# Gate and up of a SwiGLU block as a 2x2 block product in seven products (Strassen–Winograd) instead of eight, with every low part on VectorE

## What is computed

```
x: 2048 x 512, float32; attention weights Wq 512 x (16 x 32), Wk and Wv 512 x (16 x 8); gate and up 1792 x 512; down 512 x 1792
xn = (x - mean) / sqrt(var + eps)                       per token
q, k, v = xn Wq + bq, xn Wk + bk, xn Wv + bv
attn    = softmax over e of (q k^T)/4, per token, 16 x 16; s = attn v
nx = xn * rsqrt(mean(xn^2) + eps) * ln_w
g  = silu( ( silu(nx gate^T) * (nx up^T) ) down^T )
out = x + s * g
```

## Time and profile before

| | |
|---|---|
| time, median of three runs | 522.2 us (522.16 to 522.37) |
| span of the profiled execution | 520.4 us |
| instructions | 6685 |
| PE busy (matmuls) | 507.2 us, 97%, 2320 matmuls |
| DVE busy | 374.8 us, 72% |
| ACT busy | 195.1 us, 37% |
| HBM read and written | 25.56 and 7.34 MB |
| mean granted TensorE clock | 0.997 of full speed |

### The profile page before, as it was taken

How to read it: one execution, slowest core, us unless ns; L and a number is a source line. 1 busy time by engine, 2 the same in 40 slices (tenths; PEclk the granted TensorE clock), 3 DMA queues, 4 the chain that set the end, 5 groups by cost and what they waited for, 6 DMA issues and landing times.

```text
span 520.4 us, 6685 instructions
## 1 busy us (share of the span) xinstructions
PE 507.2 (97%) x2320; PEld 424.8 (82%) x2320; DVE 374.8 (72%) x542; ACT 195.1 (37%) x373; POOL 27.5 (5%) x41
## 2 busy tenths in 40 slices
PE   6999999999999999999999999999999999999993
PEld 5888888888888888888888888888888888888882
DVE  6899756876278653886569797686775867588777
ACT  4857862124311234114276575211332114221311
POOL 5030010200102000010000000000000000000000
PEclk9999999999999999999999999999999999999998
DMA  8823350000400004000043212201031010300312
GB/s 269 287 82 102 97 186 0 1 1 2 161 0 0 0 0 161 0 0 0 0 161 102 81 42 81 82 0 40 0 128 74 0 40 0 122 0 1 112 50 81
DMA packets 15168, 33.11 MB, mean 64 GB/s; under 512 B 1456, under 2 KB 2736, under 8 KB 14384
## 3 DMA queue, kind: packets, MB, share of 16 engines
q1 hardware_dynamic: 13200, 22.42, 13.5%
q0 software_dynamic: 1952, 10.49, 5.8%
HBM read 25.56 MB, written 7.34 MB: 63 GB/s over the span
## 4 chain that ended last, share of the span: by engine, by line
PE 95%; DVE 2%; ACT 1%; DMA 1%; SPq 0%; issue 0%; DVEq 0%; ACTq 0%
PE gate_ps L283 29%; PE up_ps L283 29%; PE y_ps L283 29%; PE aux_ps L283 6%; PE aux_ps L367 1%; DMA raw<-gate 1%; DVE raw L702 1%; DVE y_part L697 0%; ACT zT_hi L536 0%; DVE y_part L687 0%; SPq L172 0%; ACT raw L437 0%; DVE h_lo L746 0%; DVE h L738 0%; ACT y_part L526 0%
## 5 line engine op out<-in xcount | busy, mean ns | idle before, releaser
L471 ACT ACTIVATE h_hi<-h 128x512 fp32r<-128x512 f32 x56 | 35.4, 632 | 173.9 <-DVE h L738 159.4
L738 DVE TENSOR_TENSOR h<-h,up_ps 128x512 f32<-128x512 f32 x56 | 38.4, 687 | 79.4 <-PE up_ps L283 76.8
L283 PE MATMUL y_ps<-down_hi,h_hi 128*128 128x512 f32 x224 | 88.4, 395 | 0.3 <-DVE h_lo L746 0.3
L283 PE MATMUL y_ps<-down_hi,h_lo 128*128 128x512 f32 x224 | 87.7, 391 | 0.0
L283 PE MATMUL up_ps<-zT_hi,up_hi 128*128 128x512 f32 x224 | 87.5, 391 | 0.0
L283 PE MATMUL y_ps<-down_lo,h_hi 128*128 128x512 f32 x224 | 87.5, 390 | 0.0
L283 PE MATMUL up_ps<-zT_hi,up_lo 128*128 128x512 f32 x224 | 87.3, 390 | 0.0
L283 PE MATMUL up_ps<-zT_lo,up_hi 128*128 128x512 f32 x224 | 87.2, 389 | 0.0
L283 PE MATMUL gate_ps<-zT_hi,gate_hi 128*128 128x512 f32 x224 | 83.3, 389 | 1.0 <-ACT zT_hi L536 1.0
L283 PE MATMUL gate_ps<-zT_hi,gate_lo 128*128 128x512 f32 x224 | 83.3, 389 | 0.0
L283 PE MATMUL gate_ps<-zT_lo,gate_hi 128*128 128x512 f32 x224 | 83.3, 389 | 0.0
(11 more groups left out here) (75 smaller groups left out, 603.2 us busy)
## 6 DMA issues: line engine op xcount, KB each, us to landing
z<-x POOLq DMA_DIRECT2D x4, 1024.0 KB, 6.9
raw<-x SPq DMA_DIRECT2D x4, 1024.0 KB, 5.5
out<-raw SPq DMA_DIRECT2D x16, 256.0 KB, 2.0
raw<-gate SPq DMA_DIRECT2D x14, 256.0 KB, 2.7
raw<-up SPq DMA_DIRECT2D x14, 256.0 KB, 2.7
raw<-down SPq DMA_DIRECT2D x14, 256.0 KB, 2.7
zT_kept<-zT_raw POOLq DMA_DIRECT2D x3, 1024.0 KB, 8.5
zT_raw<-zT_kept POOLq DMA_DIRECT2D x3, 1024.0 KB, 5.1
```

The source lines that it names most:

```text
L283: last = pe.matmul(acc, lhsT, rhs, start=start and n == 0, stop=stop and n == len(pairs) - 1)
L471: act.activation(h_hi[:, i % 2, :], h[:, i % 2, :], ACT.Copy).then_inc(h_hi_done, 1)
L738: dve.tensor_tensor(h[:, i % 2, :], h[:, i % 2, :], up_ps[:, i % 2, :], ALU.mult)\
```

## The change

The kernel is rewritten around another tiling of gate and up. Two blocks (1024 tokens) are taken together as a pair, and K = 512 inputs are split in two halves. For one step of 128 hidden units the four products of gate and up with the two blocks are one 2x2 block matrix product, weights (gate, up) x (K half 1, half 2) by inputs (K half 1, half 2) x (block 0, block 1). It is made in the Winograd form, with seven products of 6 matmuls instead of eight, from operands W: A11, A12, A22 and the four sums S1 to S4, and Z: B11, B21, B12, B22 and the sums T1 to T4.

- A **group** is one step of one pair: `m1` to `m7`, 42 matmuls of 512 columns, where before 48 stood, and one down product of 12. There are 2 pairs x 14 = 28 groups. PE's order in a group is m1, m5, m6, m2, m7, a down product, m4, m3.
- The sums of products are made in PSUM where one product can accumulate on another. Where the copy is needed twice it is carried by ScalarE: `seed` copies the bank of m1 to the bank in which m2 accumulates, `take_u2` copies the bank after m6, `take_u3` after m7. VectorE adds what is left: `c22` (u3, up of block 1) and `c12` (u2, gate of block 1), then `times_up0`, `times_up1`. So a group has, beside two silus, three copies on ScalarE and two additions on VectorE.
- The four weight sums are made on VectorE (`sums`, 4 x 128x256 a step), with their high parts on ScalarE (`hi_s`, 1024 wide) and low parts on VectorE (`lo_s`); A11, A12, A22 likewise (`hi_a`, `lo_a`, 768 wide). Pair 0 makes them once, each step's are stored to HBM (`w_kept`, 1.8 MB a step, `wd_kept`, 0.5 MB a step), and pair 1 loads them.
- The input sums T are made for each pair on VectorE (`t_add`, 4 x 128x1024, `t_lo`, 4 x 128x1024), with `t_hi` on ScalarE.
- `y_ps` has four banks, one block's y over all 14 steps. So h of block 1 is kept in SBUF (`h_kept`), and its 14 down products come later. There are 56 down products in all ("items"), as before. Item 13 and those of block 1 of pair 0 (items 14 to 26) stand between the pairs, in the **middle stretch**, together with the transposes and q/k/v products of pair 1. Those of block 1 of pair 1 stand at the end.
- q/k/v of pair 0 are made at the start, all eight tiles together. VectorE's attention is one chain of 208 steps, of which fixed shares are put in each group (2+2 in pair 0, 5+3 in pair 1) and between the items of the middle stretch.
- `wq`'s columns are summed on GpSimd. There is no loop: each engine's program is written out.

What counts on TensorE: 1176 + 672 matmuls of 512 columns where 1344 + 672 stood, the same 192 of 384 columns, and the same 64 transposes of 128.

The diff, cut to what is spoken of below:

```diff
-            def one_block(blk, phase, first=False, last=False):
-                for i in range(S):
-                    gate_product(blk, phase, i)
-                    up_product(blk, phase, i)
-                    ...
-                    down_product(blk, phase, i - 1)
+            for index in range(JJ):                       # PE, pair 0
+                if index == JJ - 1:
+                    m6(0); m5(0); m7(0)
+                qkv_product(index)                        # waits for qkv_out
+                ...
+            for g in range(1, NI):
+                m1(g); m5(g); m6(g); m2(g); m7(g)
+                down_product(g - 1)
+                m4(g); m3(g)
+            for j in range(3):
+                next_tile(j)
+            down_product(NI - 1)
+            for j in range(3, JJ):
+                next_tile(j)                              # waits for z_raw_done
+            for u in range(NI, 2 * NI - 1):
+                down_product(u)                           # item NI waits for y_done
+                if u >= NI + 3 and u - NI - 3 < JJ:
+                    qkv_product(JJ + u - NI - 3)
+            ...
+            for u in range(ITEMS - NI - 1, ITEMS - 2):
+                down_product(u)
...
+            for j in range(3, JJ):                        # ACT, middle stretch
+                z_raw_tile(1, j - 1)                      # waits for z_lo_done
+                z_hi_tile(1, j)
+            z_raw_tile(1, JJ - 1)
+            for j in range(J):
+                y_out(0, j)
+            for u in range(NI + 1, 2 * NI):
+                h_hi_part(u)                              # waits for items 0 to u - 2
+                if 2 <= u - NI < 5:
+                    t_hi(1, u - NI - 2)
...
+            h_lo_part(NI)                                 # DVE, middle stretch
+            for j in range(JJ):
+                z_lo_tile(1, j)
+            h_lo_part(NI + 1)
+            for n in range(4):
+                t_add(1, n)
+            for n in range(3):
+                t_lo(1, n)
+                attention(2)
+                if n:
+                    h_lo_part(NI + 1 + n)
+            for index in range(JJ, 2 * JJ):
+                qkv_take(index)                           # waits for qkv_done
+                h_lo_part(NI + 4 + index - JJ)
+                attention(BURST_SHARES[index - JJ])
+            for j in range(J):
+                finish(0, j)
+            h_lo_part(2 * NI - 2)
...
+            for g in range(NI, GROUPS):                   # DVE, pair 1
+                if g > NI:
+                    c12(g - 1); times_up1(g - 1)
+                    h_lo_part(item_of(1, 0, g - 1 - NI))
+                attention(shares[g][0])                   # 5 steps
+                c22(g)
+                attention(shares[g][1])                   # 3 steps
+                if g == NI + 6:
+                    for j in range(J):
+                        finish(1, j)
+                times_up0(g)
...
+            for u in range(ITEMS - NI + 3 + J, ITEMS):    # DVE, end
+                attention(4)
+                h_lo_part(u)
```

More of the change, by code:

```diff
@@ L411, in _, with product @@
-            pe.wait_ge(const_done, 3)
+            def product(acc, g, m, start=False):
+                wi, zi = m
+                for c in range(2):
+                    w_h, w_l = (w_ops[:, g % 2, s, wi, c * P:(c + 1) * P] for s in range(2))
+                    pe.matmul(acc, w_h, z_hi[:, zi, c, :], start=start and c == 0, stop=False,
+                              skip_group_check=True)
+                    pe.matmul(acc, w_h, z_lo[:, zi, c, :], start=False, stop=False, skip_group_check=True)
+                    end = pe.matmul(acc, w_l, z_hi[:, zi, c, :], start=False, stop=c == 1,
+                                    skip_group_check=True)
+                return end
@@ L532, in _ @@
[L532 removed]
+            act.wait_ge(lnw_in, 16)
+            scale(0, (0,))
+            hi_a(0, 0, 2, 1)
             for j in range(J):
[L535 to L543 removed]
@@ new lines, in _ @@
+            z_raw_tile(0, JJ - 1)
+            hi_s(0)
+            for n in range(3):
+                t_hi(0, n)
+            scale(1, (1,))
+            hi_a(1, 2, 3, 4)
+            take_u2(0)
+            t_hi(0, 3)
+            take_u3(0)
+            hi_wd(0)
+            hi_s(1)
+            h_hi_part(0)
+            scale(2, (0, 1))
+            for g in range(1, NI):
+                if g >= 2:
+                    seed(g)
+                silu1(g - 1)
+                if g + 1 < NI:
+                    hi_a(g + 1, 0, 3, a_pieces(g + 1))
+                take_u2(g)
+                if g >= 2:
+                    silu0(g)
+                take_u3(g)
+                hi_wd(g)
+                if g + 1 < NI:
+                    hi_s(g + 1)
+                if g + 2 < NI:
+                    scale(g + 2, (0, 1))
+                exps(exps_in(g))
+                h_hi_part(g)
@@ new lines, in _ @@
+            first_tiles(J, between)
+            lo_a(0, 2, 3, 3)
+            sums(0)
+            qkv_take(0)
+            z_lo_tile(0, J)
+            z_lo_tile(0, J + 1)
+            qkv_take(1)
+            z_lo_tile(0, J + 2)
+            z_lo_tile(0, J + 3)
+            lo_s(0)
+            qkv_take(2)
+            for n in range(4):
+                t_add(0, n)
+            qkv_take(3)
+            for n in range(3):
+                t_lo(0, n)
+                qkv_take(4 + n)
+            lo_a(1, 2, 3, 4)
```

1338 lines of the change are left out of this document (790 added, 548 removed).

## The result

The changed kernel takes 573.1 us (median of 4 runs, 571.5 to 574.5) against 522.2 for the kernel before in the same comparison (521.9 to 522.4): 1.097 times the time, 95% interval 1.095 to 1.099. It is slower, though TensorE (PE) does 190 matmuls fewer, 168 of them of products and the rest small ones.

What follows compares the result with a forecast made beforehand. PE's matmuls were taken to bound the kernel, busy 97% of the span. 219.1 (through pair 0) + 105.5 + 179.9 + 52.6 + 5.2 = 562.3 us, with the clock 572.3; median 1.8 above: 574 us, range 556 to 598.

Steps and rivals of the forecast that it cites:

- start and group 0 end at: From kernel start through group 0: ends at 57.4 us, with 13.0 us of PE waiting.
- groups 2 to 13: Pair 0's full groups: 12.24 us of PE work each, plus 2.5 us for table loads and heavy attention shares.
- middle: Stretch between the pairs: 105.5 us, 47 us over its PE work of 58.5.
- pair 1: Fourteen groups of 12.24 us plus 8.5 us of waits, 6.0 of them at finish: 179.9 us.
- end: Last 15 down products: 40.8 us of work plus waits on VectorE, 52.6 us.
- clock: Idle of about 5 us halves PE's clock; five pauses that long cost 10 us, of 0 to 25.
- queues: Each engine's written order, followed, sets when PE's items start; 85.6 us of waits in all.
- pauses of 1.65 ahead of items 18 to 25: Middle stretch: h_lo stands behind qkv_take, so each of eight items waits 1.65 us and takes 6.5.
- PE runs through: Rival: the queues don't hold as read, waits stay under 43 us in sum; 517 us, chance 0.06.
- Traffic: Rival: HBM traffic reaches only 230 GB/s, so 13 groups last 13.6 us each; 590 us, chance 0.06.
- low clock over whole thin stretches: Rival: the start's q/k/v and items 14 to 18 take twice their length on the path; 595 us, chance 0.10.
- `finish` would be absorbed: Rival: long pauses leave the clock up and pair 1's groups absorb finish; 560 us, chance 0.15.

Runs made afterwards that it cites:

- e12_fill: Changed kernel plus useless identity transposes in the start's and middle's pauses, and one 512-column matmul over bank 2 ahead of item 26; 565.7 us, ratio 1.083.
- the swap: Changed kernel with h_lo of items 18 to 25 put ahead of qkv_take on VectorE in the middle stretch; 563.7 us, ratio 1.081.
- the new order: Changed kernel with the whole middle stretch reordered on ScalarE and VectorE, same instructions; 537.3 us, ratio 1.027.
- e9_order: Seven more order edits on the 524.0 us kernel, which had the middle, pair 1's finish, end and start reordered; 514.0 us, ratio 0.985.
- e4_middle: Changed kernel with only the middle stretch reordered on ScalarE and VectorE, same instructions; 537.3 us, ratio 1.027.

## Why the prediction was right, term by term

| term | forecast | measured | |
|---|---|---|---|
| start and group 0 end at | 57.4 | 61.4 | 5.9 us of slow matmuls, forecast in the term clock |
| group 1 | 12.3 | 13.5 | clock at 0.5 for 3.4 us in it |
| groups 2 to 13 | 149.4 | 147.8 | the waits of 2.5 were 0.9 |
| middle | 105.5 | 107.2 | 7.7 us of slow matmuls in it |
| pair 1 | 179.9 | 180.3 | |
| end | 52.6 | 56.5 | 3.1 of it one wait not seen, some 4 slow matmuls |
| tail | 5.2 | 4.7 | |
| clock | 10 | 7.2 where it was tried | inside the rows above |
| span | 572.3 | 571.4 | |

That the span came within 1 us is in part luck. PE's work, the start up to the first product and the tail make 458, 13.7 and 4.7 us; the other 95 us are some 21 of extra time in slow matmuls and 74 of waits. The forecast had 10 and 85.6. Two errors of 11 us cancel, and they hang together: where a down product waits for VectorE, slow matmuls ahead of it only fill its pause. With the clock up (e12_fill) items 14, 16 and 17 start 17.1, 30.5 and 41.1 us behind the end of pair 0, and 17.1, 30.5 and 41.5 in the changed kernel. The forecast added the clock's price on top of such pauses.

The **queues** were read rightly. Rows of PE in the middle, with the releasers that the forecast named; it put items 14, 16 and 17 at T = 18.25, 32.65 and 41.95, and with T = 0 at 222.7 they came at 17.1, 30.5 and 41.5, item 26 at 102.6 (forecast 102.75):

```profile
239.77 0.77 PE L456 MATMUL y_ps<-wd_ops,h_hi 128*128 128x512 f32 x1 [4.99 <-ACT xz L700]
253.23 0.79 PE L456 MATMUL y_ps<-wd_ops,h_hi 128*128 128x512 f32 x1 [5.89 <-DVE h_lo L945]
264.15 0.79 PE L456 MATMUL y_ps<-wd_ops,h_hi 128*128 128x512 f32 x1 [5.98 <-DVE h_lo L945]
272.20 0.50 PE L456 MATMUL y_ps<-wd_ops,h_hi 128*128 128x512 f32 x1 [1.31 <-DVE h_lo L945]
```

The arrival times are right within 2.2 us, the pauses only roughly: 5.1, 6.1 and 6.1 us before items 14, 16 and 17, where 6.2, 8.5 and 6.6 were forecast. Two runs bear the cause out: the swap took 8.8 us from the middle, the new order 35 of the 47 that the forecast put above its work. The pauses of 1.65 ahead of items 18 to 25 measured 1.47. The claim that the product removed is gained where groups are full was shown by the eighth product put back.

**Mis-sized or missed.** The *clock* term rested on five pauses of 5 us or more, since "about 5 us of idle bring it down". That step was wrong. The trace has eleven falls to 0.5. Four begin inside the pauses before items 16, 17 and 26 and at `finish`, 3.2, 2.6, 2.0 and 4.8 us after PE stopped. Six go with pauses of 2.3 to 4.0 us (the clock is 0.66 on average from 41 to 46 us, after a pause of 2.9). One, at 233.5, begins 1.3 us before the pause of item 14, in the second of two pauses of 1.2 us with four transposes between them:

```profile
231.82 0.66 PE L494 MATMUL gu_ps<-ident,xz 128*128 128x128 f32 x4 [1.17 <-ACT raw L643]
233.67 1.12 PE L494 MATMUL gu_ps<-ident,xz 128*128 128x128 f32 x4 [1.19 <-ACT raw L643]
...
233.00:233.50 0.50, 0.00 (x0) 0.00 (x0) 0.00 (x0) 0.48 (x1) 0.00 (x0) 1.00 0.63 262
233.50:234.00 0.50, 0.33 (x2) 0.34 (x3) 0.00 (x0) 0.50 (x2) 0.00 (x0) 0.51 0.87 356
```

The falls make some 21 us of extra matmul time, of which the runs with transposes give back 7 at the start and in the middle; what those at `finish` and at the end cost net was not tried. The forecast's 10 is near such a net price by luck of two errors: twice the falls, each worth less than assumed, since much of the slow time lay beside VectorE's queue. The *end* missed one wait: the load of item 51 stood on SP behind four stores and a load that waits for them.

```profile
536.77 3.09 SPq L271 DMA_DIRECT2D out<-xz  x4
542.50 0.39 SPq L266 DMA_DIRECT2D xz<-x  x1
542.94 3.89 SPq L259 DMA_DIRECT2D wd_ops<-wd_kept  x3
```

The prediction took each down weight as there in time and read no order of SP's queue at the end. That step was incomplete; the first mend of it showed how much hangs on it (item 51 behind the stores and the load waits 3.6 us; item 52 behind the 1 MB load 2.1; in e9_order, where item 51 is behind the four stores alone, 0.9 by its row at 490.67). VectorE's *busy time* was put at some 450 us and is 426.6; nothing rested on it.

**The rivals.** That PE runs through was the wrong side for this kernel, but its condition was right: below 43 us of waits it wins, and e9_order, with the same work and some 27 us in pauses, does. Traffic of 262 GB/s bound nothing: groups 2 to 13 took 12.3 us each, against 12.24 of PE's work. Of low clock over whole thin stretches, the middle had 0.86 on average and the start 0.89, not 0.5; but the fall at 233.5 belongs to a thin stretch and not to one long pause. That `finish` would be absorbed fell with the pause of 5.4 us behind `seed`.

**Open.** How much of the remaining 32 us between PE's busy time and the span of e9_order can go. The order of the kernel before was not worked over in the same way; with 97% busy and pauses of 3.4 us in all it has little of that kind to give.

## What to carry to other kernels

Removing work from the bounding engine is worth its full time only where that engine was full and stays full; price the stretches in which the others then come too late one by one, from each queue's written order, and mend that order before judging the algorithm: here the same instructions took 573 and 514 us. An operation that is ready belongs ahead of one that still waits in the same queue, on the DMA-issuing engine too. After a wait is taken away look for the next one behind it; until that was done the gains were 13 of 22 us hoped for.

## What the runs showed of the hardware

Of the eleven falls of the clock to 1.2 GHz in the changed kernel seven began 2.0 to 4.8 us into a pause, three up to 1.5 us after PE had resumed, and one in the second of two pauses of 1.2 us with only four transposes between them; the shortest single pause with a fall was 2.3 us. The length of a pause alone doesn't decide it: a pause of 2.16 us (by its row) at 276 us of e4_middle left the clock at 1.00 from 276 to 282, and one of the same length ahead of the same item in e9_order, at 263, was followed by 0.57 from 265 to 269.

VectorE instructions that read two operands from SBUF took up to 2.3 times as long while GpSimd worked in SBUF (0.69 to 1.58 us), and GpSimd's own 512-wide operation took from 1.1 to 2.15 us in the same kernel; VectorE's reductions, with one operand, kept their mean of 1217 ns (one beside GpSimd, at 477.03, took 1.21 us). A matmul with a start over 128 columns of a bank changes how later accumulation treats the other 384.
